# An attention and mixture-of-experts kernel: SyncE's own order of work, new strings of turns, and routed weight loads that wait for a number from the routing table

## The chip, the cores and the metric

One Trainium2 chip, one core. The metric is the device time of one execution in microseconds (us), the median of several runs. The kernel is one program with one instruction stream for each engine: TensorE (PE), VectorE (DVE), ScalarE (ACT), GpSimd (POOL) and SyncE (SP), which issues nearly all DMAs.

## The reference

Batch 8, 512 tokens, width 512, 16 query heads and 4 key/value heads of 32, then 16 routed experts (the best 2 of each token) and 2 shared experts of inner width 256.

```python
x = x + _layernorm(_L0_attn_ref(_layernorm(x), Wq, bq, Wk, bk, Wv, bv, Wo, bo))   # rotary, causal softmax
x = x + _layernorm(_L0_ffn_ref(_layernorm(x), ...))
# inside _L0_ffn_ref
aff = sigmoid(x @ wa)
topk_p, topk_i = top_k(aff, 2); topk_p = topk_p / sum(topk_p)
combine = sum(one_hot(topk_i, E) * topk_p[..., None], axis=2)
routed = einsum('bsed,bse->bsd', experts(x, rg, rgb, rw1, rb1, rw2, rb2), combine)
shared = sum(experts(x, sg, sgb, sw1, sb1, sw2, sb2), axis=2)
return x + shared + routed
# an expert: w2( gelu(x @ g + gb) * (x @ w1 + b1) ) + b2
```

## The kernel before

**Attention.** A planner, `plan_attention`, writes one list of steps for all eight batches (2,780 steps, some 341 for each batch in the middle). Every engine walks the same list and does its share of each step, waiting on semaphores. The order comes from threads that are merged by strings: each letter gives one thread a turn. For each batch there are two passes, `FIRST` (head groups 0 and 1 are finished; maxima of groups 2 and 3 of this batch) and `SECOND` (head groups 2 and 3; maxima of groups 0 and 1 of the next batch). `h` is the thread of scores and values, `m` the row maxima and sums, `k` keys, queries and the rows of a coming batch, `v` its values, `t` the tail of the batch before (output projection, layer norms, router logits). The first batch has strings of its own ahead of it (`OPEN`, `NEXT`), and the last batch uses `EIGHTH`, `LAST` and `CLOSE`.

SP walks the list too, in its order, one wait after the other, and issues:
- `qmove`, `kmove`: the rotated and split queries and keys from `st` to `Qs` and `Ks` (six DMAs each).
- `mTlo`: two rows of maxima of one head group from `mT` to `Qs` (L1119), then the sums to DRAM, `rt_scratch` (L1124). The second score matmul group of a pass cannot start without these rows.
- `rbc`: the same sums back from `rt_scratch`, broadcast, to `rd` (L1133). It first waits until the write to `rt_scratch` has landed. `rd` is needed by `ymul` (L1617), which scales the finished values of a head.
- `x1`, `xn`, `xtlo`: stores of the tail's rows (L1140, L1145, L1158); `xn` also starts the load of the next tile's `xr` (L1069).

In the list, around the change of pass in batch 3 (the positions repeat every 341 steps in the other middle batches): `x1` 1260, `rbc` of group 2 at 1264, `xn` 1268, `xtlo` 1283, `mTlo` of group 3 at 1284, `rbc` of group 3 at 1290, `qmove` 1291, `x1` 1302, `ymul` of the second pass 1387.

**Shared experts and routing.** `plan_moe` interleaves the shared experts' matmuls with the routing. On DVE the routing steps `route(9)` to `route(12)` stand as one block between two shared units: the next `up` unit's DVE step (L1918) comes behind them. `route(11)` ends with the table `tab`: for each of the 79 slots of 128 tokens the expert (row 0), the place in the ring of weights (row 1), whether the weights must be loaded (row 2, 1 at the first slot of an expert) and a number for the scatter (row 3).

**Routed slots.** The ring has `NSLOT` = 5 places, each with the 1.5 MB of one expert. For each slot ACT and DVE split a quarter of the first weights at a time into two parts (`cut`, L1472 and L1962), PE multiplies (L2140), and the second product (`rdown`, L2374) reads the ring as well. SP issues two conditional DMAs a slot in `fetch_w(j)`; both count on the semaphore `d_wr[j % NSLOT]` whether they load or not:

```python
if j >= NSLOT:
    w.wait_ge(rdown_pe, j - NSLOT + 1)
ex = e.value_load(tab[0:1, 0, j:j + 1], ...)      # and sl, fl in the same way
e.dma_start(ring[:, bass.ds(sl, 1), 0:2048], w1[...], cond=fl).then_inc(d_wr[j % NSLOT], 16)
```

Slot j's `cut` comes two slots ahead of its `rdown` in every engine's order. Behind the routed slots the last three groups of shared tiles and the final layer norms follow.

Of the kernel before, what the change touches and what calls it, by code (L numbers as in the profile page):

```python
# [9 lines left out]
I32 = mybir.dt.int32  # L10
# [7 lines left out]
NT = B * T // 128  # L18
NS = 2 * NT + E - 1
NSLOT = 5  # L20
NCUT = 6
NPUT = NT // 2
GB = 5
# [92 lines left out]
def on_diagonal(qh, kc):  # L116
# [5 lines left out]

OPEN = ("rrrrrrrrrrrrrrrrrrkrrkrhhrrhhrkhrrhkkkkkkkkkrrkrkhk")
NEXT = ("kmmmmkkmmkkmmkmkmmmmmkkmmkkkmkkkmkmkmmkkmmmmkkmkmmmmkmkkmmkmmkmkkmkkkkmmk")
FIRST = ("hhmvkmkmhkkmkmhttvkmhtvkkmkmtkkkmktkmmmktkhvmhtttvmhtkhhkhhmkhkmhttkkhttmtkkkhmtkkmmhmkk"
         "tkmthttkkmhhmtvkkhvmhhmmhthhkttmhkvth")
SECOND = ("hhmthmtthkmhtktkmtthmtkktmkttkmtmtmkkhmkkmthhkhmmkktmmhhmhtkhkmmmhttkkmthkkmtktkkmmmhkhh"
          "tmhmmkmhkhmkhthtkmtkhkktkkkkhkkhthk")
EIGHTH = ("khhmkmhhhkhkkmhmtmmhthhtkhkhkmkhtmthkhtmkmhmmhmmkmkthkkkmmkkththtmhkhkkhtkmmtmhththkhtth"
          "hkhkkmktmkhhmttkmtkkhmmhttktmmtmktmkkhmhhmtt")  # L130
LAST = ("hthhktktkkkhtktthtthhtkhhhhkkkhthhtththttttkttttkhkkhhhkkkkhkkkkkhhththhkhhkkhkthkthhk")
CLOSE = ("ttkttttttkktkktttkkttttttttktttktkkkttktttttttktttttkttttktttktkttttkttttttkttktttkktttk"
         "tktttttttttktttt")


def merge(turns, drain, threads):

    for c in turns:
        if c in threads:
            next(threads[c], None)  # L140
    live = [threads[c] for c in drain if c in threads]
    while live:
        live = [g for g in live if next(g, "over") != "over"]


def plan_attention():
# [294 lines left out]
    for b in range(B):  # L441
# [22 lines left out]
            threads["t"] = tails  # L464
        merge(SECOND if more else LAST, "hmkt" if more else "h", threads)
    merge(CLOSE, "tk", {"t": tails, "k": weights})
    return P


# [184 lines left out]
def program(nc, x, wq, bq, wk, bk, wv, bv, wo, bo, wa, w1, w2, b1c, b2k, rb, trig, trigk, out):  # L654
# [14 lines left out]
    with ctx:  # L669
# [3 lines left out]
        def sems(name, n):  # L673
            return [sem(f"{name}{i}") for i in range(n)]
# [112 lines left out]
        with fctx:  # L787
            def sb2(name, shape, dt=F32):
                return fctx.enter_context(nc.sbuf_tensor(name, shape, dt))
# [58 lines left out]
            assert free + 24576 <= end_at - 7 * 4096  # L848
            cT = sb2("cT", [80, 2, 128], F32R)
            pos = sb2("pos", [128, 2, NT], I32)  # L850
            tab = sb2("tab", [1, 4, 80], I32)
            vb = sb2("vb", [1, 168])
            ohs = sb2("ohs", [48, 80])
            ohj = sb2("ohj", [128, 2, 128], F32R)
# [28 lines left out]
        def hbuf(n):  # L883
            k = 4 * ((n // 4 - GB) % 2) + n % 4
            return hT[:, k // 4, k % 4, :, :] if n < N1 else hT3[:, 7 - k, :, :]

        def xbuf(g):
            return xt[:, g % 2 if g < GB else (g - GB) % 2, :, :]

# [6 lines left out]
        hT_hi, hT_lo, comb_lo = sem("hT_hi"), sem("hT_lo"), sem("comb_lo")  # L896
        cT_pe, cT_act, down_pe, zs_dve = sem("cT_pe"), sem("cT_act"), sem("down_pe"), sem("zs_dve")
        d_zs, d_zi = sems("d_zs", 3), sem("d_zi")
        d_wr, d_xr2, d_ys = sems("d_wr", NSLOT), sems("d_xr2", 4), sems("d_ys", 4)
        take_pe, xg_act, xg_dve, ohj_dve = sem("take_pe"), sem("xg_act"), sem("xg_dve"), sem("ohj_dve")  # L900
        cut_act, cut_dve, cut_pe = sem("cut_act"), sem("cut_dve"), sem("cut_pe")
        rup_pe, rgl_act, rh_dve = sem("rup_pe"), sem("rgl_act"), sem("rh_dve")
# [148 lines left out]
        def _(e):  # L1051
# [31 lines left out]
                    for i in range(4):  # L1083
                        e.dma_start(xbuf(g)[:, i, :].bitcast(F32), XT[4 * g + i]).then_inc(d_xt[g % 2], 16)

            for step in PA.steps:
                kind, a = step[0], step[1:]
                if kind == "xload" and a[0] > 0:
                    b, = a
# [114 lines left out]

            def fetch_w(j):
                if j < NS:
                    w.wait_ge(route_dve, 10)
                    if j >= NSLOT:
                        w.wait_ge(rdown_pe, j - NSLOT + 1)
                    elif j > 1:  # L1210
                        w.wait_ge(zs_dve, N1)
                        w.wait_ge(hT_lo, N1)
                    elif j:
                        w.wait_ge(up_pe, ups(N1 - 1))
                        w.wait_ge(down_pe, N1 - 4)
                    ex = e.value_load(tab[0:1, 0, j:j + 1], min_val=0, max_val=E - 1)
                    sl = e.value_load(tab[0:1, 1, j:j + 1], min_val=0, max_val=NSLOT - 1)
                    fl = e.value_load(tab[0:1, 2, j:j + 1], min_val=0, max_val=1)
                    e.dma_start(ring[:, bass.ds(sl, 1), 0:2048], w1[bass.ds(ex + SH, 1)], cond=fl).then_inc(d_wr[j % NSLOT], 16)  # L1219
                    e.dma_start(ring[:, bass.ds(sl, 1), 2048:3072], w2[bass.ds(ex + SH, 1)], cond=fl).then_inc(d_wr[j % NSLOT], 16)  # L1220

            for step in PM.steps:
                kind, n = step
                if kind == "up" and n == N1:
                    load(GB + 1)
                elif kind == "up" and n % 4 == 3 and not N1 - 5 <= n < N1:
                    load(n // 4 + 2)
                elif kind == "down" and n < N1:
                    w.wait_ge(zs_dve, n + 1)
                    if n == 0:  # L1230
                        for v in (Z, XN):
                            for pad in (NT, NT + 1):
                                e.dma_start(rows_of(v, pad), zs[:, 0, :]).then_inc(d_zs[0], 16)
                    e.dma_start(rows_of(Z, n), zs[:, n % 3, :]).then_inc(d_zs[n % 3], 16)
                    load_rows(n + 4)
                    if n == 8:
                        e.dma_start(Z[128 * N1:128 * NT, :].rearrange("(p r) d -> p (r d)", p=128),
                                    XN[128 * N1:128 * NT, :].rearrange("(p r) d -> p (r d)", p=128)).then_inc(d_zi, 16)
                    if n == N1 - 6:
                        w.wait_ge(put_pe, NPUT)  # L1240
                        w.wait_ge(pl_dve, 1)
                        fetch_w(0)
                    if n == N1 - 4:
                        fetch_w(1)
                elif kind == "take":
                    if n == 0:
                        load(GB)
                        for j in range(2, NSLOT):
                            fetch_w(j)
                elif kind == "rdown":  # L1250
                    fetch_w(n + NSLOT)
                elif kind == "fx":
                    fetch_x1(n)
                elif kind == "fz":
                    for i in range(4):
                        w.wait_ge(d_ys[i], 16 * len(range(i, NS, 4)))
                    p = PAIR[n]
                    pair_free(n)
                    if n < GB:
                        e.dma_start(group(zf[p]), Z_g[n]).then_inc(d_rows[p], 16)  # L1260
                    else:
                        e.dma_start(zf[p][:, :, :], tiles_of(Z, n)).then_inc(d_rows[p], 16)
                elif kind == "fadd":
                    p = PAIR[n]
                    for h in range(2):
                        w.wait_ge(f_out, PM.ends.out[4 * n + 2 * h + 1])
                        e.dma_start(out_g[n][:, 1024 * h:1024 * h + 1024], group(zf[p], 2 * h, 2 * h + 2)).then_inc(d_fo[p], 16)
                elif kind == "tadd":
                    w.wait_ge(f_out, PM.ends.out[n])
                    e.dma_start(rows_of(out_rows, n), buffer_of(n)[0]).then_inc(d_fo[PAIR[n // 4]], 16)  # L1270

            for i in range(NSLOT):
                w.wait_ge(d_wr[i], 32 * len(range(i, NS, NSLOT)))
            for p, had in PM.ends.of_pair.items():
                e.wait_ge(d_fo[p], sum(64 if v >= GB else 32 for v in had))

# [2 lines left out]
        def _(e):  # L1279
# [156 lines left out]
            for step in PM.steps:  # L1436
# [28 lines left out]
                    place = e.value_load(tab[0:1, 1, n:n + 1], min_val=0, max_val=NSLOT - 1)  # L1465
                elif kind == "cut":
                    j, k = divmod(n, 4)
                    w.wait_ge(d_wr[j % NSLOT], 32 * (j // NSLOT + 1))
                    w.wait_ge(zs_dve, N1)
                    if n >= NCUT:  # L1470
                        w.wait_ge(cut_pe, n - NCUT + 1)
# [30 lines left out]
        def _(e):  # L1502
# [271 lines left out]
            def route(j):  # L1774
# [76 lines left out]
                elif j == 11:  # L1851
                    src, dst = flip
                    done()
                    e.tensor_scalar(sm[0:1, 448:528], src, -1.0, None, ALU.add).then_inc(dve_own, chain.up())
                    for k in range(1, (NSLOT + E - 2) // NSLOT + 1):
                        done()
                        e.tensor_scalar(dst, src, float(NSLOT * k + 1), -float(NSLOT), ALU.is_ge, ALU.mult).then_inc(dve_own, chain.up())
                        done()
                        e.tensor_tensor(sm[0:1, 448:528], sm[0:1, 448:528], dst, ALU.add).then_inc(
                            *((dve_own, chain.up()) if k + 1 < (NSLOT + E - 2) // NSLOT + 1 else (route_dve, 1)))  # L1860
                    w.wait_ge(route_dve, 6)
                    e.tensor_copy(tab[0:1, 0, :], ej[0:1, :]).then_inc(route_dve, 1)
                    e.tensor_copy(tab[0:1, 1, :], sm[0:1, 448:528]).then_inc(route_dve, 1)
                    e.tensor_copy(tab[0:1, 2, :], fg).then_inc(route_dve, 1)
                    e.scalar_tensor_tensor(tab[0:1, 3, 1:80], fg[:, 1:80], 16.0, vb[0:1, 1:80], ALU.mult, ALU.add).then_inc(route_dve, 1)

            def stats(tiles):
                for t in tiles:
# [107 lines left out]
        def _(e):  # L1976
# [21 lines left out]
            for step in PA.steps:  # L1998
# [29 lines left out]
                elif kind in ("ln1", "x1"):  # L2028
# [37 lines left out]
                   allow_small_or_imprecise_dtypes=True).then_inc(io_pool, 1)  # L2066
            w.wait_ge(io_pool, 7)
            e.iota(io[:, 0:1280], pattern=[[1, 80], [0, E]], base=0, channel_multiplier=0,
                   allow_small_or_imprecise_dtypes=True).then_inc(io_pool, 1)

            w.wait_ge(io_pool, 8)
# [366 lines left out]
```

## Time and profile before

| what | value |
|---|---|
| median of 3 runs | 1628.55 us (1628.39 to 1633.31) |
| the profiled execution | 1629.32 us |
| its span | 1627.6 us, so 1.7 us lie around it |
| mean granted TensorE clock | 0.926 |
| PE busy | 1448.1 us, 89% |
| DVE, ACT, POOL busy | 1055.3, 981.2, 549.5 us |

PE is the busiest engine by far, so a wait costs what it keeps PE idle, and a granted clock under 1.00 makes PE's work longer. The stages by time from the start: attention up to about 880 us, shared experts with the routing to 1051, routed slots to 1490, the remaining shared tiles and the layer norms to the end.

### The profile page before, as it was taken

The page shows a single profiled execution, that of the slowest core. Times are in us where ns is not written, and L with a number is a line of the kernel's source. Part 1 is how long each engine was busy: PE and PEld are TensorE (multiplying, and loading weights), DVE is VectorE, ACT ScalarE, POOL GpSimd, SP SyncE. Part 2 cuts the span into 40 slices and gives each one's busy share as a digit, 9 for nine tenths or more (in the row PEclk, how much of TensorE's full clock was granted, in tenths as well). Part 3 has the DMA queues.
Part 4 walks back from the last instruction along what each step waited for, and adds up shares of the span by engine and source line. Part 5 has one row for each costly group of instructions (what it writes and reads, how often), then busy time and mean ns, then how long its engine had stood idle before and what let it go on. Part 6 is the DMA issues. An engine that isn't in the chain of part 4 may idle for free. (4 is left out here: it accounts for less than half of the span.)

```text
span 1627.6 us, 24759 instructions
## 1 busy us (share of the span) xinstructions
PE 1448.1 (89%) x7066; PEld 1014.0 (62%) x7067; DVE 1055.3 (65%) x2115; ACT 981.2 (60%) x2423; POOL 549.5 (34%) x781
## 2 busy tenths in 40 slices
PE   4699989888898988988788889999899999999986
PEld 4464756655565655753467678776666666666774
DVE  4566767686776768766545675376677766674366
ACT  3678767686776777867533111276677766775233
POOL 2122332323223232322312034145455555553024
PEclk9687989989799898988889889999999999999998
DMA  5453555655555564553534432546867566664756
GB/s 164 65 92 61 121 127 114 148 104 115 116 110 132 102 131 97 99 127 95 188 128 177 142 130 104 185 107 149 238 158 173 120 170 132 139 130 54 294 218 223
DMA packets 103695, 222.93 MB, mean 137 GB/s; under 512 B 14228, under 2 KB 40342, under 8 KB 99672
## 3 DMA queue, kind: packets, MB, share of 16 engines
q1 hardware_dynamic: 85864, 179.92, 41.1%
q0 software_dynamic: 17696, 41.43, 13.3%
q8 instruction: 58, 0.95, 0.3%
q14 instruction: 77, 0.63, 0.1%
HBM read 219.20 MB, written 72.35 MB: 179 GB/s over the span
## 5 line engine op out<-in xcount | busy, mean ns | idle before, releaser
L1591 DVE TENSOR_REDUCE mr<-bank 128x1 f32<-128x512 f32 (+3 forms) x352 | 214.6, 634 | 119.4 <-PE bank L2211 118.0
L1343 ACT ACTIVATE bank<-bank,mr 128x384 f32<-128x384 f32 (+3 forms) x512 | 255.1, 501 | 41.6 <-DVE mr L1591 40.2
L1360 ACT ACTIVATE P<-bank 128x512 f32<-128x512 f32 x320 | 181.5, 596 | 91.6 <-PE bank L2225 90.2
L1962 DVE TENSOR_TENSOR cut<-ring,cut 128x512 fp32r<-128x512 f32 x316 | 197.1, 685 | 57.3 <-ACT cut L1472 54.0
L2140 PE MATMUL bank<-cut,xg 128*128 128x512 f32 x632 | 205.4, 406 | 16.2 <-DVE cut L1962 16.2
L1472 ACT ACTIVATE cut<-ring 128x512 fp32r x316 | 173.6, 623 | 55.3 <-DMA ring<-in_w 52.0
L2209 PE MATMUL bank<-Ks,Qs 96*128 96x384 f32 (+3 forms) x512 | 171.0, 403 | 36.9 <-DMA Qs<-st 17.4
L2026 POOL TENSOR_SCALAR_AFFINE_SELECT P<-P 128x256 f32<-128x256 f32 (+1 forms) x192 | 94.0, 496 | 290.3 <-ACT P L1360 287.7
L2225 PE MATMUL bank<-Qs,Ks 98*128 98x512 f32 x320 | 153.9, 514 | 38.5 <-DMA Qs<-mT 26.9
L2140 PE MATMUL bank<-xt,ws 128*128 128x512 f32 x768 | 182.2, 395 | 0.8 <-DVE hb L1723 0.8
L2123 POOL DMA_INDIRECT z_scratch<-wst,pl x79 | 126.3, 1598 | 133.5 <-ACT wst L1493 120.2
L2140 PEld LDWEIGHTS bank<-xt,ws 128*128 128x128 f32 x768 | 145.3, 191 | 32.8 <-issue 1.4
L2209 PEld LDWEIGHTS bank<-Ks,Qs 96*128 96x128 f32 x512 | 104.6, 218 | 92.9 <-ACT P L1360 29.5
L2374 PE MATMUL bank<-ring,hr 128*128 x316 | 148.8, 593 | 0.7 <-ACT hr L1485 0.7
L2140 PEld LDWEIGHTS bank<-cut,xg 128*128 128x128 f32 x632 | 113.9, 190 | 39.9 <-DVE cut L1962 16.4
L2140 PE MATMUL bank<-cut,xgl 128*128 128x512 f32 x316 | 124.6, 394 | 0.0
L2225 PEld LDWEIGHTS bank<-Qs,Ks 98*128 98x128 f32 x320 | 67.1, 221 | 80.4 <-DMA Qs<-mT 28.6
L2089 POOL DMA_INDIRECT xs<-xn_scratch,pl x79 | 94.3, 1193 | 63.6 <-PE bank L2346 25.5
L2140 PE MATMUL bank<-wo_s,yn 128*128 128x512 f32 x384 | 113.3, 419 | 0.0
L2140 PE MATMUL bank<-xT,wq_s 128*128 128x512 f32 x384 | 113.1, 419 | 0.0
L1343 ACT ACTIVATION_READ_ACCUMULATOR bank<-bank,mr 128x1 f32 x512 | 106.3, 208 | 0.0
L2140 PE MATMUL bank<-ws,hT 128*128 128x512 f32 x384 | 102.4, 418 | 0.0
(247 smaller groups left out, 2525.7 us busy)
## 6 DMA issues: line engine op xcount, KB each, us to landing
ring<-in_w SPq DMA_DIRECT2D x79, 1024.0 KB
ring<-in_w SPq DMA_DIRECT2D x79, 512.0 KB
Qs<-st SPq DMA_DIRECT2D x192, 128.0 KB, 4.8
xt<-xt_scratch SPq DMA_DIRECT2D x32, 512.0 KB, 6.3
xt_scratch<-xt SPq DMA_DIRECT2D x30, 512.0 KB, 3.1
xin<-in_x SPq DMA_DIRECT2D x8, 1024.0 KB, 7.2
rd<-rt_scratch SPq DMA_DIRECT2D x64, 128.0 KB, 2.6
xf<-x_scratch SPq DMA_DIRECT2D x8, 1024.0 KB, 9.3
```

Of the source, the lines that this page charges most:

```text
L1343: m = e.activation(ps[:, o * k:o * k + k], ps[:, o * k:o * k + k], ACT.Exp, scale=-1.0, bias=mr[:, G % 2, c:c + 1], accum_out=se[:, G % 2, ...
L1360: e.activation(Pt[:, p, :], bank[PA.bank[step]][:, :], ACT.Exp, scale=-1.0).then_inc(s_exp, 1)
L1472: e.activation(cut[n % NCUT][:, 0:1, :], ring[:, bass.ds(place, 1), 512 * k:512 * k + 512], ACT.Copy).then_inc(cut_act, 1)
L1591: e.tensor_reduce(mr[:, G % 2, 0:16].rearrange("p (h i) -> p h i", i=4)[:, h:h + n, i:i + 1], bank[PA.bank["max", b, p, j]][:, 0:n * k].re ...
L1962: e.tensor_tensor(cut[n % NCUT][:, 1:2, :], ring[:, bass.ds(place, 1), 512 * k:512 * k + 512], cut[n % NCUT][:, 0:1, :], ALU.subtract).the ...
L2026: e.affine_select(out=v, in_=v, compare_op=ALU.is_ge, fill=0.0, base=0, pattern=pat, channel_multiplier=-1).then_inc(s_sel, 1)
L2089: e.indirect_dma_start(xs[:, j % 4, :], None, XN, bass.IndirectOffsetOnAxis(ap=pl[:, j, 1:2], axis=0)).then_inc(d_xr2[j % 4], 16)
L2123: e.indirect_dma_start(Z, bass.IndirectOffsetOnAxis(ap=pl[:, n, 1:2], axis=0), yo[:, o, :], None, compute_op=ALU.add).then_inc(d_ys[o], 16)
L2140: m = e.matmul(ps, lhs(a_, k), rhs(b_, k), start=first and k == 0 and j == 0, stop=last and k == n - 1 and j == 2)
L2209: e.matmul(ps[:, o * k:o * k + k], Qs[0:96, 4 * g + h + o, i * 128:(i + 1) * 128], Ks[0:96, b % 2, g, 0:k], start=o == 0, stop=False)
L2225: e.matmul(bank[PA.bank[step]][:, :].rearrange("p (h q) -> p h q", h=nh), Ks[0:98, b % 2, g, kc * 128:(kc + 1) * 128], Qs[0:98, h:h + nh, ...
L2374: m = e.matmul(ps[:, :].rearrange("p (o n) -> p o n", o=1), hr[:, q, 128 * k:128 * k + 128], ring[:, bass.ds(reg[n], 1), 2048 + 512 * k:20 ...
```

## The change

SP gets a list of its own, `P.queue`: the planner's steps sorted by position, where `x1` counts as 10 positions later, `xn` 2, `xtlo` 4 and `rbc` 31. Only SP uses it. `FIRST` and `SECOND` get other strings with the same number of each letter (125 and 123 turns). A slot's load now waits for a number from a fifth row of `tab`: how many slots the experts up to five before this one take, at least 1; beside it for slot j - 12 (`AHEAD` = 12). All calls of `fetch_w` from slot 2 stand together at the first `take`. The semaphores are twelve, seven of them reused from `ld` (they stand at 16 already). DVE makes the fifth row at the end of `route(11)`.

```diff
+AHEAD = 12
-FIRST = ("hhmvkmkmhkkmkmhttvkmhtvkkmkmtkkkmktkmmmktkhvmhtttvmhtkhhkhhmkhkmhttkkhttmtkkkhmtkkmmhmkk"
-         "tkmthttkkmhhmtvkkhvmhhmmhthhkttmhkvth")
-SECOND = ("hhmthmtthkmhtktkmtthmtkktmkttkmtmtmkkhmkkmthhkhmmkktmmhhmhtkhkmmmhttkkmthkkmtktkkmmmhkhh"
-          "tmhmmkmhkhmkhthtkmtkhkktkkkkhkkhthk")
+FIRST = ("httthmkkmvhmkmkmvkhkhtvtmktkkmmkhhmtkmmkttmkkkmhtvmhkmkhkvhhhhktmtkktktvmkthvmmktmhtkmkk"
+         "mhmmtkhkhtmhkthmtkhmhkhhtkvtmtkthkhkh")
+SECOND = ("hmhthmktmkthmkttmtttkkmthkkmmmtmhthmttmmtmkhthkmthhktmhkkmkmmkmkhmkhmhttmkmtktkmthkhkhmm"
+          "hkhhmkhkkmhkthkmtkkhtkkkhkhkkttkhkk")
+LATER = {"x1": 10, "xn": 2, "xtlo": 4, "rbc": 31}
+    P.queue = [s for _, _, s in sorted((n + LATER.get(s[0], 0), n, s) for n, s in enumerate(P.steps))]
...
-            for step in PA.steps:
+            for step in PA.queue:
...
+        def landed_w(j):
+            return 32 * (j // AHEAD + 1) + 16 * (j % AHEAD < 7)
...
-                    w.wait_ge(route_dve, 10)
+                    w.wait_ge(route_dve, 11)
                     if j >= NSLOT:
-                        w.wait_ge(rdown_pe, j - NSLOT + 1)
+                        spent = e.value_load(tab[0:1, 4, j:j + 1], min_val=1, max_val=NS - 1)
+                        if j >= AHEAD:
+                            w.wait_ge(rdown_pe, j - AHEAD + 1)
...
+                    if j >= NSLOT:
+                        e.wait_ge(rdown_pe, spent)
...
-                        for j in range(2, NSLOT):
+                        for j in range(2, NS):
                             fetch_w(j)
-                elif kind == "rdown":
-                    fetch_w(n + NSLOT)
...
-                    w.wait_ge(d_wr[j % NSLOT], 32 * (j // NSLOT + 1))
+                    w.wait_ge(d_wr[j % AHEAD], landed_w(j))
...
+                    gone = v3(cmp_[0:1, 0:1280])
+                    w.wait_ge(io_pool, 9)
+                    e.tensor_tensor(gone, ej[0:1, :].rearrange("p (j o) -> p j o", o=1).to_broadcast([1, 80, E]),
+                                    fifth[:, :].rearrange("p (o e) -> p o e", o=1).to_broadcast([1, 80, E]), ALU.is_ge).then_inc(dve_own, chain.up())
+                    done()
+                    e.tensor_tensor(gone, gone, te[0:1, :].rearrange("p (o e) -> p o e", o=1).to_broadcast([1, 80, E]),
+                                    ALU.mult).then_inc(dve_own, chain.up())
+                    done()
+                    e.tensor_reduce(dst.rearrange("p (j o) -> p j o", o=1), gone, AX.X, ALU.add).then_inc(dve_own, chain.up())
+                    done()
+                    e.tensor_scalar(tab[0:1, 4, :], dst, 1.0, None, ALU.max).then_inc(route_dve, 1)
...
+            w.wait_ge(io_pool, 8)
+            e.iota(fifth[:, :], pattern=[[1, E]], base=NSLOT, channel_multiplier=0,
                    allow_small_or_imprecise_dtypes=True).then_inc(io_pool, 1)
```

## Rows read from the trace of the kernel before

**Rows 1.** The page: busy time of each engine.

```profile
PE 1448.1 (89%) x7066; PEld 1014.0 (62%) x7067; DVE 1055.3 (65%) x2115; ACT 981.2 (60%) x2423; POOL 549.5 (34%) x781
```

**Rows 2.** Stretches (one batch; shared experts): us; busy by engine; granted clock; DMA share; GB/s.

```profile
382.80:480.40 97.60, 87.11 (x498) 57.83 (x497) 70.24 (x144) 72.00 (x205) 29.33 (x56) 0.90 0.55 118
...
951.00:1051.00 100.00, 99.11 (x466) 81.60 (x465) 49.63 (x67) 14.43 (x31) 31.90 (x18) 0.98 0.41 140
```

**Rows 3.** PE's waits, 0 to 880 us: total us, times, longest.

```profile
PE bank L2225 <- DMA Qs<-mT: 26.9, 6, 5.1
...
PE bank L2209 <- ACT P L1360: 17.1, 29, 1.9
```

**Rows 4.** PE's only wait, 1055 to 1490 us.

```profile
PE bank L2140 <- DVE cut L1962: 16.2, 13, 2.9
```

**Rows 5.** PE's timeline, batch 3: start us, us, in brackets idle before.

```profile
408.75 0.79 PE L2225 MATMUL bank<-Qs,Ks 98*128 98x512 f32 x1 [5.09 <-DMA Qs<-mT]
...
418.03 0.39 PE L2225 MATMUL bank<-Qs,Ks 98*128 98x512 f32 x1
...
429.72 0.79 PE L2209 MATMUL bank<-Ks,Qs 96*128 96x512 f32 x1 [1.32 <-ACT P L1360]
```

**Rows 6.** SP's timeline at the same place: start us, us.

```profile
397.38 0.42 SPq L1140 DMA_DIRECT2D x_scratch<-x  x1
400.53 2.26 SPq L1133 DMA_DIRECT2D rd<-rt_scratch  x2
402.84 0.42 SPq L1145 DMA_DIRECT2D xn_scratch<-xn  x1
...
404.37 1.63 SPq L1119 DMA_DIRECT2D Qs<-mT  x2
...
408.89 0.79 SPq L1133 DMA_DIRECT2D rd<-rt_scratch  x2
```

**Rows 7.** DVE's timeline at the same place, and the next pass's `ymul`.

```profile
400.40 0.27 DVE L1603 TENSOR_TENSOR mT<-bank,mT 16x128 fp32r<-16x128 f32 x1
...
434.23 0.69 DVE L1617 TENSOR_TENSOR flat<-bank,rd 128x512 f32<-128x512 f32 x1 [0.17 <-PE bank L2245]
```

**Rows 8.** Stretches of 2 us behind the wait, columns as in Rows 2.

```profile
410.00:412.00 2.00, 2.00 (x7) 1.61 (x7) 0.69 (x1) 1.48 (x7) 1.49 (x5) 0.50 0.68 209
412.00:414.00 2.00, 2.00 (x12) 1.64 (x11) 0.69 (x1) 2.00 (x9) 0.88 (x2) 0.99 1.16 141
```

**Rows 9.** SP's timeline of `fetch_w`: the first DMA of slots 3, 4, 5, 9.

```profile
1057.24 0.08 SPq L1219 DMA_DIRECT2D ring<-in_w  x1
...
1059.88 0.08 SPq L1219 DMA_DIRECT2D ring<-in_w  x1
...
1071.63 0.08 SPq L1219 DMA_DIRECT2D ring<-in_w  x1
...
1093.07 0.36 SPq L1219 DMA_DIRECT2D ring<-in_w  x1
```

**Rows 10.** The chain that ended last, routed slots: start us, us.

```profile
1075.36 2.75 PE bank L2140 x12
1080.72 2.75 PE bank L2140 x12
...
1093.83 7.42 DMA ring<-in_w
...
1165.78 10.34 DMA ring<-in_w
```

**Rows 11.** DVE's timeline in the routing block.

```profile
941.00 1.49 DVE L1833 TENSOR_REDUCE sm<-fl 128x80 f32<-128x1280 f32 x1
942.52 0.20 DVE L1835 TENSOR_SCALAR sm<-sm 128x80 f32<-128x80 f32 x1
...
948.51 0.73 DVE L1918 SCALAR_TENSOR_TENSOR hb<-bank,b_s,gl 128x512 f32<-128x512 f32 x1
```

**Rows 12.** PE's timeline behind the routing block.

```profile
950.11 0.80 PE L2339 MATMUL bank<-b_s,cT 80*128 80x512 f32 x1 [5.40 <-ACT cT L1457]
```

More of the change, by code:

```diff
@@ L850, in program @@
             pos = sb2("pos", [128, 2, NT], I32)
-            tab = sb2("tab", [1, 4, 80], I32)
+            tab = sb2("tab", [1, 5, 80], I32)
+            fifth = sb2("fifth", [1, E])
             vb = sb2("vb", [1, 168])
@@ L898, in program @@
         d_zs, d_zi = sems("d_zs", 3), sem("d_zi")
-        d_wr, d_xr2, d_ys = sems("d_wr", NSLOT), sems("d_xr2", 4), sems("d_ys", 4)
+        d_wr, d_xr2, d_ys = ld[1:8] + sems("d_wr", AHEAD - 7), sems("d_xr2", 4), sems("d_ys", 4)
         take_pe, xg_act, xg_dve, ohj_dve = sem("take_pe"), sem("xg_act"), sem("xg_dve"), sem("ohj_dve")
@@ L1218, in fetch_w @@
                     fl = e.value_load(tab[0:1, 2, j:j + 1], min_val=0, max_val=1)
-                    e.dma_start(ring[:, bass.ds(sl, 1), 0:2048], w1[bass.ds(ex + SH, 1)], cond=fl).then_inc(d_wr[j % NSLOT], 16)
-                    e.dma_start(ring[:, bass.ds(sl, 1), 2048:3072], w2[bass.ds(ex + SH, 1)], cond=fl).then_inc(d_wr[j % NSLOT], 16)
+                    if j >= NSLOT:
+                        e.wait_ge(rdown_pe, spent)
+                    e.dma_start(ring[:, bass.ds(sl, 1), 0:2048], w1[bass.ds(ex + SH, 1)], cond=fl).then_inc(d_wr[j % AHEAD], 16)
+                    e.dma_start(ring[:, bass.ds(sl, 1), 2048:3072], w2[bass.ds(ex + SH, 1)], cond=fl).then_inc(d_wr[j % AHEAD], 16)
             for step in PM.steps:
@@ L1270, in _ @@
                     e.dma_start(rows_of(out_rows, n), buffer_of(n)[0]).then_inc(d_fo[PAIR[n // 4]], 16)
-            for i in range(NSLOT):
-                w.wait_ge(d_wr[i], 32 * len(range(i, NS, NSLOT)))
+            for i in range(AHEAD):
+                w.wait_ge(d_wr[i], landed_w(max(range(i, NS, AHEAD))))
             for p, had in PM.ends.of_pair.items():
@@ L2068, in _ @@
             e.iota(io[:, 0:1280], pattern=[[1, 80], [0, E]], base=0, channel_multiplier=0,
+                   allow_small_or_imprecise_dtypes=True).then_inc(io_pool, 1)
+            w.wait_ge(io_pool, 8)
+            e.iota(fifth[:, :], pattern=[[1, E]], base=NSLOT, channel_multiplier=0,
                    allow_small_or_imprecise_dtypes=True).then_inc(io_pool, 1)
```

## The prediction

> **What bounds the kernel now.** First the busy table: PE is busy 1448.1 us [rows 1], some 400 us more than the next engine. So a change can pay in two ways: less time in which PE stands still, or PE at its higher clock. Next the stretches: one middle batch of attention takes 97.6 us, PE works 87.1 of them, and the granted clock is 0.90, so part of the batch runs at 1.2 instead of 2.4 GHz; while the shared experts run, PE is busy 99.1 of 100 us [rows 2]. The list of PE's waits then gives the reasons. In attention the largest is one wait for a DMA, the rows of maxima: 26.9 us in six waits, one in each of batches 1 to 6; many short ones for ACT follow [rows 3]. In the routed slots there is only one reason: PE waits for a `cut`, 16.2 us in 13 waits, none over 2.9 [rows 4], and the chain there runs through the load of the weights, 7.42 and 10.34 us in the rows shown [rows 10]. Those are the two places that the change touches; what they hold is 43 us, 2.6%.
>
> **The wait in attention.** PE's score matmul starts at 408.75 after 5.09 us of nothing [rows 5]. It needs the maxima that SP sends at L1119. DVE has them ready at 400.40 + 0.27 = 400.67 [rows 7], but SP issues at 404.37 [rows 6]. In between SP stands in an earlier step: after `x1` at 397.38 it waits for the sums' write to land, issues `rbc` from 400.53 for 2.26 us, then `xn`, the next `xr` and `xtlo` [rows 6]. That is a queue held up by a step nobody needs yet: the `ymul` that wants what `rbc` brings runs at 434.23 [rows 7].
>
> **SP's own order.** `rbc` of group 2 moves from position 1264 to 1295, `xtlo` from 1283 to 1287, `xn` from 1268 to 1270, and `mTlo` stays at 1284. So `rbc` and `xtlo` go behind it, and only `x1` and `xn` (with its `xr`) stay ahead; both were ready, since SP issued them without a pause. The maxima can leave at 400.7 in place of 404.37: 3.7 us earlier, 22 us over six batches. From issue to the matmul it takes 408.75 - 404.37 = 4.4 us, so PE would go on at 405.1, while it ran dry at 408.75 - 5.09 = 403.7; 1.4 us of the wait would be left. This is where the new strings come in: of `FIRST`'s 28 `m` turns the last six stand at turns 90, 91, 98, 103, 107 and 116 in place of 97, 100, 107, 110, 111 and 119. A turn is about half a batch over 125, 0.39 us, so the maxima are ready 1.2 to 3.5 us earlier against the rest of the pass. That is about the 1.4 left. I count the whole 26.9 as gone. Bounds: 22 us if the strings add nothing, and 0 if PE meets another wait at the same place.
>
> What is moved back: a position is 97.6 / 341 = 0.29 us, so `rbc` goes 31 positions or 9 us later. Before, the later of the pair is issued at 408.89 and its `ymul` runs at 434.23 [rows 6, 7]: 25 us, less some 4 for landing as for the maxima. 9 us later still fits. It now stands behind `qmove` at 1291, whose six DMAs hold SP a few us more; they fit as well. `x1` is 10 positions or 3 us later, and the next `x1` of the tail, which reuses its buffer, is 42 positions on. `xr` starts earlier than before, as it no longer stands behind `rbc`. I count nothing for these; if `rbc`'s cover went, `ymul` would hold PE's next values (a rival below).
>
> **The clock behind the wait.** Between 410 and 412 PE is busy all the time at clock 0.50, and from 412 at 0.99 [rows 8]; the 512-column matmul takes 0.79 us at 408.75 and 0.39 at 418.03 [rows 5]. So from 408.75 to 412, 3.25 us, PE does 1.6 us worth of work: 9.8 us over six batches if nothing takes the wait's place. But a wait of only 1.32 us at 429.72 also leaves PE at 0.79 us a matmul [rows 5], so short gaps matter too, and the new order may move a slow stretch rather than end it. I take half, 4.9 us; bounds 0 and 9.8.
>
> **The rest of the strings.** The number of each letter is unchanged, so no work is added. A batch has 97.6 - 87.1 = 10.5 us of standing still; without the 5.1 there are 5.4 left, 32 us over six batches, partly waits for ACT's `P` (17.1 us in 29) [rows 2, 3]. The strings can shorten or lengthen these, and no row says which. I take zero; bounds 16 us better (half of what is left) and 27 us worse (all that was won).
>
> **The routed loads.** Before, slot j's load waits for `rdown` j - 5, and `cut` j comes two slots ahead of `rdown` j: the load has less than three slots, at a pitch of 1080.72 - 1075.36 = 5.36 us, and needs up to 10.34 [rows 10]. After, it waits for `rdown` j - 12, seven slots or 37.5 us earlier. The largest wait is 2.9 us, so each goes. The table's number binds only where four experts in a row take fewer than 12 slots together; the mean is 79 / 16 = 4.9 slots each, so about 20. Where it binds, a lead of six slots already beats the 2.9 us. The first load, slot 9 (1093.07, a DMA of 0.36 us beside 0.08 for those that load nothing), now only waits for `rdown` 0 as slot 5 does (1071.63), with four fetches behind that. One fetch takes SP 2.64 us with three register loads [rows 9]; with four at most 2.64 x 4 / 3 = 3.5, so slot 9 is issued at 1086, 7 us earlier, and SP keeps under the pitch. Behind the waiting `fetch_w` on SP there stand only other fetches and, after slot 78, the loads for the end, which wait for the last `rdown` anyway. Gain 16.2 us [rows 4]; bounds 12 (a quarter of the waits stays) and 16.2. The Trainium skill, page "DMA: Bandwidth & Descriptors", section "Queues, rings and completion order", says that the 16 DMA engines take packets from the queues in turn; by that rule an early load would slow POOL's gathers and scatters just as a late one does, and a bunch of loads would slow them more. No wait of PE for a gather is among its waits here [rows 4], so the sum by the rule is the same unless gathers become late.
>
> **The fifth row of the table.** Three more passes over 1,280 elements on DVE and one short one. The same size takes 1.49 us and a short one 0.20 [rows 11]; partitions don't shorten it, the elements on each do. 3 x 1.49 + 0.20 + three gaps of 0.03 = 4.8 us. They stand ahead of the `hb` of the next shared unit at 948.51 [rows 11]. ACT's split waits for `hb`, ACT's `cT` is queued behind the split, and PE has stood 5.40 us at 950.11 waiting for that `cT` [rows 12]. So nothing covers them, and behind them PE is full [rows 2]: the 4.8 us are added to the end. Bounds 4.8 and 6 (PE stays at half clock a little longer). The iota on POOL is tiny and early; SP's wait for the eleventh step is met long before slot 0.
>
> **The sum.** 1629.3 (the profiled execution) - 26.9 - 4.9 - 16.2 + 4.8 = 1586.1. The median of the runs is 0.8 below the profiled execution, so 1585.5.
>
> **The rivals.**
> - As forecast, 0.55. Its own range is 1573 to 1600: SP's part alone and no clock gives 1595; the full clock 1581.
> - The strings pay more, 0.17: half of the short waits go (16) and the clock comes back in full (4.9 more), 1565. For it: two strings rewritten whole. Against: the six long waits are the only ones over 3 us in the middle batches.
> - Another wait takes the place of the six, 0.15: PE arrives earlier at the scores and finds ACT's `P` or the queries late. Half of the 26.9 and no clock: 1585.5 + 13.5 + 4.9 = 1604. For it: the short waits for ACT in the rows [rows 3].
> - Attention gains nothing, 0.05: 1628.5 - 16.2 + 4.8 = 1617. The same kind of result, some 1602, if the loads alone don't do what they say.
> - No change within 0.3% (1623.7 to 1633.4; 0.3% is about what a measurement of this kernel can tell from none), 0.04: attention loses 7 to 16 us by new short waits.
> - Slower, 0.04: `rbc` comes too late. Its place is `ymul`, which frees the bank for PE's next values, in 14 passes. It decides if SP's queue is so held that `rbc` is over 20 us later than before. From 1585.5 it takes 48 us, 3.4 us of PE's time a pass, to pass 1633.4. Against it stand the 25 us of cover.
>
> Faster by over 0.3%: 0.92; within: 0.04; slower: 0.04. The range takes in most of the second and the third case: 1560 to 1612.
>
> **What would show it.** PE's wait for `Qs<-mT` gone or under 1 us each; SP issues L1119 within 0.5 us of DVE's L1603; L1133 comes behind L1119. A batch of 91 to 93 us in place of 97.6. Clock over 0.92 in the middle batches. No PE wait for `cut` after the first slots, 79 slots at 5.36 us. PE's wait at the routing block 10 us in place of 5.4. I am wrong if a new wait of 2 us or more a batch appears in attention, above all for `P`, `y` or `st`, or if DVE's block is hidden.

## The result and the profile after

The changed kernel takes 1584.38 us, the median of 4 runs (1582.73 to 1586.38), against 1630.93 (1628.39 to 1634.25). The ratio is 0.971, 95% interval 0.9685 to 0.9735. The forecast was 1585.5 us. The profiled execution has a span of 1583.9 us, 43.7 less than before.

Where the time came from is read best from a few marks in both traces. The views of three lines tell when each first and last ran: `ymul` on DVE (its last one ends attention's passes), then `rdown` on PE (first and last routed slot). Of the kernel before:

```profile
L1617 DVE TENSOR_TENSOR flat<-bank,rd x32: 678/690/692, 109.7 to 828.9; 128x512 f32<-128x512 f32 x32
```
```profile
L2374 PE MATMUL bank<-ring,hr x316: 592/592/692, 1067.7 to 1503.0; 128*128 x158
```

Of the changed kernel:

```profile
L1628 DVE TENSOR_TENSOR flat<-bank,rd x32: 680/692/693, 110.8 to 798.4; 128x512 f32<-128x512 f32 x32
```
```profile
L2399 PE MATMUL bank<-ring,hr x316: 592/592/692, 1040.4 to 1458.2; 128*128 x158
```

| stretch | before | after | difference | forecast |
|---|---|---|---|---|
| start to the last `ymul` | 828.9 | 798.4 | -30.5 | -31.8 |
| to the first `rdown` | 238.8 | 242.0 | +3.2 | +4.8 |
| first to last `rdown` | 435.3 | 417.8 | -17.5 | -16.2 |
| to the end of the span | 124.6 | 125.7 | +1.1 | 0 |

Among PE's waits of the changed kernel from 0 to 880 us, `Qs<-mT` is left with one wait of 0.4 us (before, its 26.9 us led the list, [rows 3]); two of the costly rows are:

```profile
PE bank L2234 <- ACT P L1371: 17.2, 28, 5.6
...
PE bank L2242 <- DVE mr L1609: 11.8, 9, 3.4
```

SP, then DVE, at the change of pass in batch 3, which answer to [rows 6, 7]:

```profile
389.37 0.45 SPq L1149 DMA_DIRECT2D x_scratch<-x  x1
389.92 1.14 SPq L1128 DMA_DIRECT2D Qs<-mT  x2
391.16 0.52 SPq L1133 DMA_DIRECT2D rt_scratch<-rT  x1
391.87 1.21 SPq L1167 DMA_DIRECT2D xt_scratch<-xt  x1
393.18 1.17 SPq L1142 DMA_DIRECT2D rd<-rt_scratch  x2
```
```profile
388.69 0.28 DVE L1614 TENSOR_TENSOR mT<-bank,mT 16x128 fp32r<-16x128 f32 x1 [2.50 <-ACT mT L1363]
```

DVE makes the maxima ready at 388.69 + 0.28 = 388.97 here; SP issues them 0.95 us later, ahead of `rbc` (the prediction had said within 0.5 us; SP was issuing the next `xr` and `x1` just then). Before it was 3.7 us later and behind `rbc`.

Four middle batches, each from one `ymul` to the same one a batch later, show what that is worth. The columns are as in [rows 2], and the `sum` line is over all four; before:

```profile
383.90:481.51 97.61, 87.12 (x497) 57.84 (x496) 70.25 (x144) 72.01 (x205) 29.34 (x55) 0.90 0.55 118
...
sum 389.58, PE 348.08 PEld 231.70 DVE 281.09 ACT 288.30 POOL 117.33; mean PE 87.02 PEld 57.92 DVE 70.27 ACT 72.07 POOL 29.33
```

and of the changed kernel:

```profile
372.69:463.79 91.10, 86.81 (x497) 56.05 (x497) 70.38 (x143) 71.52 (x205) 29.02 (x55) 0.93 0.60 126
...
sum 364.84, PE 344.69 PEld 223.13 DVE 281.41 ACT 286.23 POOL 116.06; mean PE 86.17 PEld 55.78 DVE 70.35 ACT 71.56 POOL 29.01
```

A batch went from 97.4 to 91.2 us (the sums over four), 6.2 less, and its clock from about 0.91 to 0.93. PE stands still 5.0 us of a batch in place of 10.4, and is busy 86.2 in place of 87.0.

**A new wait.** In the last batch PE stands once where it did not before. PE, then DVE and ACT, of the changed kernel:

```profile
729.91 0.69 PE L2234 MATMUL bank<-Ks,Qs 96*128 96x384 f32 x1 [5.57 <-ACT P L1371]
```
```profile
728.02 0.69 DVE L1628 TENSOR_TENSOR flat<-bank,rd 128x512 f32<-128x512 f32 x1 [6.73 <-DMA rd<-rt_scratch]
```
```profile
728.74 0.63 ACT L1375 ACTIVATE yn<-flat 128x512 fp32r<-128x512 f32 x1 [2.87 <-DVE flat L1628]
```

PE's row names ACT's `P`, but ACT stood behind `yn`, `yn` behind DVE's `ymul`, and that waited 6.73 us for `rd`: the `rbc` that was moved. SP there:

```profile
708.32 3.82 SPq L1118 DMA_DIRECT2D Qs<-st  x6
716.94 0.36 SPq L1174 DMA_DIRECT2D wst<-in_w  x1
717.36 0.42 SPq L1175 DMA_DIRECT2D wst<-in_w  x1
717.83 0.42 SPq L1177 DMA_DIRECT2D b_s<-in_b1c  x1
718.35 1.26 SPq L1142 DMA_DIRECT2D rd<-rt_scratch  x2
```

In this batch the load of the shared experts' weights, `wload`, stands at position 2466, and `rbc` of group 0 moved from 2438 to 2469. `wload` waits until attention's first region is free, at 716.9, the last queries' landing included. So `rbc` goes out at 718.35.

The late issue is not all of it. DVE had nothing to do from 721.3 on, and `rd` landed only at 728.0, 9.7 us after its issue, where the median of this line's DMAs is 3.7 us. The 1.5 MB of `wload`, issued just ahead, were on their way: the DMA engines' share was 0.97 to 1.01 from 720 to 726.

```profile
722.00:724.00 2.00, 1.55 (x7) 0.95 (x6) 0.00 (x0) 1.22 (x5) 0.00 (x0) 1.00 1.01 271
```

No run separates the late issue from the slow landing behind the weights.

**The routing block.** DVE and PE of the changed kernel; they answer to [rows 11, 12]. PE's first row is the `cT` matmul of the unit before:

```profile
917.14 1.47 DVE L1879 TENSOR_TENSOR fl<-sm,fifth 1x1280 f32<-1x1280 f32 x1
918.64 1.48 DVE L1882 TENSOR_TENSOR fl<-fl,sm 1x1280 f32<-1x1280 f32 x1
920.16 1.47 DVE L1885 TENSOR_REDUCE sm<-fl 1x80 f32<-1x1280 f32 x1
921.67 0.19 DVE L1887 TENSOR_SCALAR tab<-sm 1x80 int32<-1x80 f32 x1
921.78 0.73 DVE L1940 SCALAR_TENSOR_TENSOR hb<-bank,b_s,gl 128x512 f32<-128x512 f32 x1
```
```profile
902.95 0.79 PE L2364 MATMUL bank<-b_s,cT 80*128 80x512 f32 x1 [3.68 <-ACT cT L1468]
...
923.39 0.80 PE L2364 MATMUL bank<-b_s,cT 80*128 80x512 f32 x1 [8.82 <-ACT cT L1468]
```

The same `cT` matmul of the unit before, in the kernel before:

```profile
934.32 0.79 PE L2339 MATMUL bank<-b_s,cT 80*128 80x512 f32 x1 [3.67 <-ACT cT L1457]
```

The four operations put 4.64 us ahead of `hb`. PE's wait grew only from 5.40 to 8.82, by 3.4, but from the one `cT` matmul to the other it is 20.44 us in place of 15.79, 4.65 more. That distance, and not the wait, is the price.

**The routed slots.** There is no PE wait for `cut` from 1055 to 1450 us; one of 2.6 us stands ahead of the first slot, as before. The chain there is PE alone, at 5.35 us a slot, and SP's fetches of slots 8 and 9 are 3.2 us apart:

```profile
1080.21 2.75 PE bank L2165 x12
1085.56 2.75 PE bank L2165 x12
```
```profile
1053.08 0.08 SPq L1232 DMA_DIRECT2D ring<-in_w  x1
...
1056.26 0.36 SPq L1232 DMA_DIRECT2D ring<-in_w  x1
```

### The profile page after: what moved, and what is told of

It is laid out like the page before. It is cut to its first block and busy times, and to the rows that moved or that the text cites. A ratio compares the mean times of both kernels' runs of the same rounds, so it can differ in the third digit from the quotient of the medians.

```text
span 1583.9 us, 24989 instructions
## 1 busy us (share of the span) xinstructions
PE 1442.1 (91%) x7066; PEld 1001.6 (63%) x7067; DVE 1061.7 (67%) x2119; ACT 983.1 (62%) x2423; POOL 549.0 (35%) x782
## 5 line engine op out<-in xcount | busy, mean ns | idle before, releaser
L2234 PE MATMUL bank<-Ks,Qs 96*128 96x384 f32 (+3 forms) x512 | 164.6, 390 | 37.2 <-ACT P L1371 17.2
L2234 PEld LDWEIGHTS bank<-Ks,Qs 96*128 96x128 f32 x512 | 98.0, 207 | 87.7 <-ACT P L1371 30.0
L1978 DVE TENSOR_TENSOR xgl<-bank,xg 128x512 fp32r<-128x512 f32 x79 | 54.7, 692 | 103.1 <-ACT xg L1474 100.9
L1504 ACT ACTIVATE wst<-bank,pl 128x512 f32<-128x512 f32 x79 | 54.4, 688 | 98.3 <-PE bank L2399 98.3
L2165 PE MATMUL bank<-wo_s,yn 128*128 128x512 f32 x384 | 108.6, 411 | 0.0
L2039 POOL TENSOR_TENSOR st<-rp,st 128x1024 fp32r<-128x1024 f32 (+1 forms) x23 | 54.3, 2362 | 155.9 <-ACT st L1343 155.9
```

Of the source, the lines that this page charges most:

```text
L2165: m = e.matmul(ps, lhs(a_, k), rhs(b_, k), start=first and k == 0 and j == 0, stop=last and k == n - 1 and j == 2)
L2234: e.matmul(ps[:, o * k:o * k + k], Qs[0:96, 4 * g + h + o, i * 128:(i + 1) * 128], Ks[0:96, b % 2, g, 0:k], start=o == 0, stop=False)
```

## The experiments

Each kernel was timed in 5 rounds beside the kernel before on the same chip; the three groups have different chips or times, so ratios are compared across groups and medians within one.

**First group: the parts alone.** (before: median 1632.61 us)

SP's own order alone:

```diff
+LATER = {"x1": 10, "xn": 2, "xtlo": 4, "rbc": 31}
+    P.queue = [s for _, _, s in sorted((n + LATER.get(s[0], 0), n, s) for n, s in enumerate(P.steps))]
-            for step in PA.steps:
+            for step in PA.queue:        # in SP's program alone
```

> The kernel before with SP's own order alone (the old strings, the old loads). Theory A, that SP's place in its queue makes the wait for the maxima: each of the six waits falls from 4 to 5 us to about 1.4, some 20 us; in the last batch rbc now stands behind the load of the shared weights and costs some 5 us of it. Sum -13 to -20 us against before, that is 0.988 to 0.992. Theory B, that the new strings are what matters and SP's order only goes with them: under 6 us, over 0.996.

Measured: 1608.77 us, 23.8 less, ratio 0.984 (0.9811 to 0.9869). That is more than theory A's 20, and far from B. The waits for the maxima did as A said: 22.5 of 26.9 us are gone.

```profile
PE bank L2228 <- DMA Qs<-mT: 4.4, 6, 1.3
```

Its four middle batches, with PE's order that of the kernel before:

```profile
376.39:469.02 92.63, 86.00 (x497) 56.68 (x496) 70.25 (x144) 71.99 (x205) 29.32 (x55) 0.93 0.58 124
...
sum 368.50, PE 341.13 PEld 224.85 DVE 280.35 ACT 287.95 POOL 117.35; mean PE 85.28 PEld 56.21 DVE 70.09 ACT 71.99 POOL 29.34
```

The same 497 matmuls keep PE busy 85.28 us a batch in place of 87.02, at 0.93 to 0.94 in place of 0.90 to 0.91. So in these two executions 1.7 us a batch came from the clock alone, some 10 us over six batches; `rbc` alone, below, shows that this does not come with every execution. The wait of the last batch is here too (5.8 us for `P`), as theory A had it.

The new strings alone:

```diff
-FIRST = ("hhmvkmkmhkkmkmhttvk...
+FIRST = ("httthmkkmvhmkmkmvkh...
```

(and `SECOND` in the same way, both as in the change)

> The kernel before with the two new strings alone. Theory A: SP still stands in rbc ahead of mTlo, so the waits for the maxima only shrink by the 1 to 3.5 us by which the m turns come earlier: -6 to -20 us, 0.988 to 0.996, and the rows of PE still show waits for Qs<-mT of 2 us or more in batches 1 to 6. Theory B: the strings alone carry attention, -25 us or more, under 0.985.

Measured: 1608.18 us, 24.4 less, ratio 0.9836 (0.981 to 0.9863). The waits shrink more than A said, to 10.0 us in six, the longest 2.6 and the mean 1.7, so 17 us are gone; and the time is more than A allowed: just under B's 25 us, and by the ratio B's. A sized the time by the waits alone, and left out the clock behind them: PE is busy 343.96 us in the four middle batches in place of 348.08, some 6 us over six. That SP's order adds nothing by itself is ruled out by the experiment before this one.

```profile
PE bank L2225 <- DMA Qs<-mT: 10.0, 6, 2.6
```

How either part shrinks the wait is read in batch 3. DVE, SP and PE with SP's order alone:

```profile
394.87 0.27 DVE L1606 TENSOR_TENSOR mT<-bank,mT 16x128 fp32r<-16x128 f32 x1
...
395.21 1.14 SPq L1122 DMA_DIRECT2D Qs<-mT  x2
...
397.66 0.50 PE L2228 MATMUL bank<-Qs,Ks 98*128 98x512 f32 x1 [0.63 <-DMA Qs<-mT]
```

and with the strings alone:

```profile
394.31 0.28 DVE L1603 TENSOR_TENSOR mT<-bank,mT 16x128 fp32r<-16x128 f32 x1 [2.50 <-ACT mT L1352]
...
398.57 1.14 SPq L1119 DMA_DIRECT2D Qs<-mT  x2
...
401.45 0.50 PE L2225 MATMUL bank<-Qs,Ks 98*128 98x512 f32 x1 [1.16 <-DMA Qs<-mT]
```

| batch 3 | before | SP's order | strings |
|---|---|---|---|
| maxima ready to SP's issue | 3.70 | 0.07 | 3.98 |
| SP's issue to the matmul | 4.38 | 2.45 | 2.88 |
| maxima ready to PE running dry | 2.99 | 1.89 | 5.70 |
| PE's wait (first two less the third) | 5.09 | 0.63 | 1.16 |

With the strings alone SP is held as long as before; the maxima are ready 2.7 us earlier against PE's work. In both kernels the rows also land 1.5 to 1.9 us faster, for which no run has a reason.

The routed part alone:

```diff
-FIRST, SECOND as in the change
+FIRST, SECOND as before
-LATER = {"x1": 10, "xn": 2, "xtlo": 4, "rbc": 31}
+LATER = {}
```

> The routed part alone (early loads and the table's fifth row), with the old strings and SP's old order. Theory A: the waits for cut go (-16 to -17.5 us) and the fifth row costs 3.4 to 4.8 us at the wait for cT: -11.5 to -14 us, 0.9915 to 0.993. PE's wait for cT is 10 us, since without the attention part PE comes to it as early as before. Rival: the gain in the routed slots depends on something else, within 6 us of before.

Measured: 1618.97 us, 13.6 less, ratio 0.9903 (0.9875 to 0.9931). The waits for `cut` are gone but for the 2.6 us ahead of the first slot, and PE's longest wait for `cT` is 8.9 us, where 10 was expected (the matmuls ahead of it were slower, see the fifth row below):

```profile
PE bank L2364 <- ACT cT L1468: 12.6, 2, 8.9
```

The changed kernel with `rbc` of the last batch in its old place:

```diff
-sorted((n + LATER.get(s[0], 0), n, s) ...
+sorted((n + (0 if s[0] == "rbc" and s[1] == B - 1 else LATER.get(s[0], 0)), n, s) ...
```

> The changed kernel, but rbc of the last batch keeps its old place in SP's list. Theory A: PE's new wait of 5.57 us at 730 us is ymul waiting for rd, which SP fetched only after its wait ahead of the shared weights' load. Gone, the time is 5 to 7 us below the changed kernel, 1577 to 1580 us, about 0.9675 of before. Rival: the wait passes to another (P, the query moves): within 2 us of the changed kernel.

Measured: 1579.73 us, ratio 0.9663 (0.9637 to 0.9689), span 1578.0 against the changed kernel's 1583.9. The longest of PE's waits for `P` at L2235 falls from 5.6 to 1.0 us, and the last `ymul` comes at 792.5 in place of 798.4, 5.9 us earlier. By the ratios (0.9663 against 0.971) and the medians the time is some 5 to 8 us below the changed kernel's. The new wait was `rbc` behind `wload`.

**Second group: the rest, one by one.** (before: median 1633.56 us)

The fifth row's passes spread over later steps (`spent_row` holds what stood in `route(11)`: part 0 the comparison, 1 the product, 2 the sum and the maximum with 1):

```diff
+            gone_at = {5: 0, 7: 1, 9: 2}
...
                 elif kind == "place":
...
+                    if n in gone_at:
+                        spent_row(gone_at[n])
```

> The changed kernel, but the three passes for the fifth row stand one by one behind later place steps (5, 7 and 9), where DVE waits about 4 us a unit for ACT. Theory A: the row's price lay in its place, between PE's matmul and the hb it needs: PE's wait of 8.8 us for cT falls to 4.2 to 5.4 and the time by 3 to 5 us, to 1579 to 1581. Rival: DVE's time is needed there as well, or PE's slower clock ahead of the block had hidden it: within 1.5 us of the changed kernel.

Measured: 1579.92 us, ratio 0.9674 (0.9644 to 0.9704; the changed kernel's is 0.971). PE's longest wait at `cT` there is 5.2 in place of 8.8, the two `cT` matmuls are 15.6 us apart in place of 20.4, and the time is some 4 to 6 us lower. Within A; the intervals of the two ratios overlap, so the third group repeats it.

```profile
PE bank L2372 <- ACT cT L1468: 8.9, 2, 5.2
```

The loads at most seven slots ahead:

```diff
-AHEAD = 12
+AHEAD = 7
```

> The changed kernel with the loads at most seven slots ahead in place of twelve: slot j's load waits for rdown j - 7, only two slots (10.7 us) earlier than in the kernel before. Theory A: the largest wait was 2.9 us, so two slots are enough: no wait for cut in the routed slots, within 1.5 us of the changed kernel. Rival: the long lead is needed where loads follow each other closely (five loads within slots 16 to 23): 3 to 8 us of waits for cut come back.

Measured: 1582.75 us, ratio 0.9694 (0.9664 to 0.9725), and the only wait for `cut` is the 2.7 us ahead of the first slot. Two slots of lead are enough; the other five pay nothing here.

Both mends:

> The changed kernel with both mends: rbc of the last batch in its old place and the fifth row's passes spread. If the two are independent: 4.7 us from the first as measured, 3 to 5 from the second, so 1575 to 1577, about 0.9645 of before. If one hides the other: 1578 or more.

Measured: 1572.91 us, ratio 0.9634 (0.9601 to 0.9667), a little below the forecast.

Only `rbc` moved, in the kernel before:

```diff
+LATER = {"rbc": 31}
```

> The kernel before with only rbc moved back by 31 positions in SP's list; x1, xn and xtlo keep their places. Theory A: rbc is the step that holds SP up ahead of mTlo; xtlo in between was ready at 400.5, when the maxima are at 400.7, so moving it adds little. Same as SP's whole order, within 3 us of its 1608.8. Rival: the stores hold SP as well, and rbc alone gives half, about 1620.

Measured: median 1609.52 us of six runs, ratio 0.9822 (0.9777 to 0.9867). One of the six took 2700 us, for which nothing here has a reason; the ratio leaves it out. The whole of SP's order gave 0.984. `rbc` is the step that matters. The stores' moves still show in the row, 9.7 us of waits against 4.4, but not in a time that this measurement can tell apart.

The clock did not follow here. 17 us of waits are gone and PE's order is the old one, as with SP's whole order, yet over the four middle batches PE is busy as long as in the kernel before (348.08):

```profile
374.12:469.52 95.40, 87.45 (x497) 58.30 (x496) 70.59 (x145) 72.06 (x205) 29.45 (x55) 0.91 0.56 120
...
sum 374.77, PE 348.81 PEld 231.57 DVE 282.50 ACT 288.12 POOL 117.76; mean PE 87.20 PEld 57.89 DVE 70.63 ACT 72.03 POOL 29.44
```

The other five times run from 1594.70 to 1611.54 us with mean clocks between 0.922 and 0.938; the trace is of the slowest of them.

**Third group: do the parts add?** (before: median 1631.69 us)

> The changed kernel once more, beside the others of this group. 0.971 of before, as measured first; its distance to the kernel with both mends is the value wanted.

Measured: 1583.20 us (1581.03 to 1586.08), ratio 0.9715 (0.9682 to 0.9748).

> The changed kernel with both mends, once more, beside the changed kernel. If the mends are independent, 8 to 10 us below it (4.7 for rbc, 4 for the row): ratio to before 0.965 to 0.966. If the 1572.9 of the first time was luck, under 5 us below it.

Measured: 1572.46 us (1571.28 to 1576.91), ratio 0.9658 (0.9624 to 0.9692), 10.7 below the changed kernel beside it. No run of the one lies within the range of the other. The mends add, and this is the fastest kernel of the case.

The kernel before with both attention parts and the old loads:

> The kernel before with both attention parts, SP's order and the strings, and the old loads. Alone the parts gave 24 us each; the changed kernel's attention ended 30.5 us earlier. Theory A, that both take away the same six waits: together 29 to 33 us, not 48, 0.980 to 0.982. Rival, that they add: 40 us or more.

Measured: 1596.16 us, 35.5 less, ratio 0.9798 (0.9766 to 0.9831). The parts gave 24 each, so 48 if they added. By the ratios it is 0.984 and 0.9836 against 0.9798. Theory A's reason holds, though by the medians its bound of 33 us was a little low. The waits for the maxima are down to 0.5 us. Attention and the routed part do add: 0.9798 times 0.9903 is 0.970, against the changed kernel's 0.971.

The early loads with the fifth row's passes spread, attention as before:

> The kernel before with the early loads and the fifth row's passes spread over later place steps; attention as before. Theory A: the waits for cut go and nothing is paid: -16 to -18 us, 0.989 to 0.990. Rival, that the row's price was no price at the end: like the routed part before, -11 to -14 us.

Measured: 1613.59 us, 18.1 less, ratio 0.9914 (0.9882 to 0.9946). The median agrees with A; the ratio would be 14 us and overlaps with the routed part alone (0.9903), so the time does not separate the two. The rows do: PE's longest wait there is 5.4 us, as in the kernel before, against 8.9.

## Why the prediction was right

**The wait for the maxima.** Right in place and cause; the size has some luck in it. SP alone was put at 22 us of waits by the 3.7 us between the maxima and their issue; measured 22.5. But in batch 3 two things that were taken as fixed moved, and partly cancel: the rows landed 1.9 us faster than in the 4.4 us of the kernel before, and PE ran dry 1.9 us behind the maxima in place of 3.0, so it stood 1.1 us longer. The strings were to add the rest; with both, 26.5 of 26.9 us are gone. That either part alone gives most of the time was not in the prediction: the 1.2 to 3.5 us of earlier `m` turns were counted only as what closes the last 1.4 us, and alone they took, with the faster landing, 17 us of the waits.

**The clock behind the wait.** "I take half, 4.9 us" fits the changed kernel: in the middle batches PE is busy 344.69 us in place of 348.08, 0.85 us a batch, so some 5 us over six. It is a term that varies, though. SP's order alone gave 1.7 us a batch, about 10 over six, all of the upper bound; `rbc` alone gave nothing. Executions of one and the same attention differ as well. Over such four batches the old attention has 348.08, 348.84 (the routed part alone) and 350.96 us (the last experiment), and the changed one 344.5 to 345.7 in seven traces and 348.62 in the one with `AHEAD` = 7. What decides how much comes back is open, so the half was a fair middle, and that it came out within 0.2 us is luck.

**What is moved back: right for the middle batches, wrong for the last.** The cover of `rbc` was worked out in batch 3 and taken for all. In the last batch `wload`, which waits for a region of memory, stands 28 positions behind `rbc`, so 31 positions carried it past. "I count nothing for these" cost 5.9 us. It is the mechanism of the rival "Slower", at one of its 14 passes.

**The rest of the strings: more than the zero that was taken.** In the four middle batches PE stands still 21.35 us less than before, and the waits for the maxima are 19.0 of that. The other 2.35 make some 3.5 us over six batches (an estimate from these rows). Against SP's order alone a middle batch is 0.9 us shorter (91.2 against 92.1): PE stands still 1.8 us less, of which 0.6 is what is left of the maxima's waits, and is busy 0.9 us more. These gains pay for a part of the last batch's loss: 26.5 + 5.1 + 3.5 - 5.9 = 29.2 against 30.5 measured, with 1.3 us that no row here places. So attention came out within 1.3 us of its forecast by errors that nearly cancel, and the total is better than its terms.

**The fifth row.** Right in mechanism and size: the passes took 4.64 us (forecast 4.8), and the distance between the two `cT` matmuls grew by 4.65. It is 20.4 to 20.5 us in all five traces with the passes inside the block and 15.5 to 15.8 in the nine others. PE's wait of 8.82 in place of the 10 forecast is no hidden work: the unit's 24 matmuls ahead of it took 8.18 us in place of 6.94. That varies with or without the passes. They took 8.28 us with the strings alone and 8.13 with both attention parts and no fifth row, and 6.95 with `AHEAD` = 7 and the fifth row, where the wait is 10.05:

```profile
923.23 0.79 PE L2364 MATMUL bank<-b_s,cT 80*128 80x512 f32 x1 [10.05 <-ACT cT L1468]
```

That the whole stretch to the first `rdown` grew by 3.2 and not by 4.65 comes from 0.9 us less ahead of these two matmuls and 0.6 less behind them, which is not explained.

**The routed loads.** All waits went, as forecast; the stretch shrank by 17.5 us against 16.2 in PE's row. It is 417.8 us in every trace with the early loads and 434.8 to 439.7 in those without. SP's fetches of slots 5 to 9, with four register loads, are 3.2 to 3.6 us apart and later ones up to 3.9 (bound 3.5), and slot 9 went out 13.6 us behind slot 5 (forecast 14). The prediction drew on the Trainium skill, "DMA: Bandwidth & Descriptors", section "Queues, rings and completion order", which says that the DMA engines take packets from the queues in turn. No run here tests in what order they take them. No PE wait for a gather shows up in the routed slots, with loads up to twelve slots ahead or seven, so the sum did not need it.

**The end.** The 1.1 us more behind the last `rdown` tell nothing. No step of the change touches that stretch, and in the fourteen traces it takes from 121.5 to 128.5 us. In this pair PE is busy 105.1 us of it in place of 102.9, at a clock of 0.91 in place of 0.93.

## What to carry to other kernels

Look in the issuing queue for a step that waits for something no one needs yet, and put what the busiest engine waits for ahead of it; here one moved step was worth about 24 us. But work out the cover at each place where the list differs, above all at the last batch, where other waits and large loads stand in the same queue. When a long wait of TensorE goes, count the slow matmuls behind it as a range from nothing to all: these runs show both. Put new table work where its engine waits anyway, since three small passes at the wrong place cost 4.6 us. And price a delay by the distance between two marks that both kernels share, not by the length of one wait, which changes with how fast the work ahead of it was.

## What the runs showed of the hardware

In these two cases the clock fell at different times within a wait. In the kernel before, PE ran dry at 403.7 us, and the clock is 0.80 from 404 to 406 and 0.50 from there:

```profile
404.00:406.00 2.00, 0.00 (x0) 0.00 (x0) 0.39 (x1) 0.06 (x1) 1.05 (x4) 0.80 0.83 216
```

In the changed kernel's new wait PE stands from 724.3 to 729.9 us, its clock is still full from 726 to 728, and then it works at half from 730 to at least 748:

```profile
726.00:728.00 2.00, 0.00 (x0) 0.00 (x0) 0.00 (x0) 0.00 (x0) 0.00 (x0) 1.00 0.09 23
730.00:732.00 2.00, 2.00 (x6) 1.04 (x6) 1.32 (x3) 1.68 (x6) 0.00 (x0) 0.50 0.00 0
...
734.00:736.00 2.00, 2.00 (x8) 0.71 (x5) 0.36 (x1) 0.94 (x3) 0.00 (x0) 0.50 0.00 0
...
746.00:748.00 2.00, 2.00 (x7) 1.29 (x5) 0.05 (x1) 1.83 (x7) 1.26 (x4) 0.50 0.62 188
```

In the kernel before, a wait of 5.09 us was followed by only 3.25 us of slow work [rows 5, 8]. The price behind a wait of much the same length thus differs by place: 1.6 us there, and here at least 3, from 730 to 736 alone, where PE is full. A short wait can be dear as well: behind the one of 1.32 us at 429.72 [rows 5], with others of 0.5 and 0.3 us near, the clock is 0.50 in every stretch of 2 us from 430 to 442.

Partitions did not change the time of a DVE pass here: 1.47 us for 1x1280 and 1.49 for 128x1280 [rows 11].
